# Attention with relative positions and a quantised feed-forward on one NeuronCore: query rows copied on chip, and two additions moved to VectorE

## The reference

```python
x = x + attention(ln(x))          # q.k/4 + rel_bias_h + rel_bias_w, softmax, times v, times Wp, plus bp
t = ln(tokens(x))
xq = round(clip(t / mean(alpha_a1), -8, 7));  wq1 = round(clip(w1 / alpha_w1, -8, 7))
h = clip(gelu(xq @ wq1.T * alpha_w1 * mean(alpha_a1) + b1), -10, 10)
hq = round(clip(h / mean(alpha_a2), -8, 7));  wq2 = round(clip(w2 / alpha_w2, -8, 7))
out = tokens(x) + (hq @ wq2.T * alpha_w2 * mean(alpha_a2) + b2)
```

## Time and profile before

| | us |
|---|---|
| median of 3 runs (lowest, highest) | 999.8 (998.39, 1002.08) |
| the profiled execution: its own time | 1000.03 |
| the profiled execution: span of the trace | 998.2 |
| a unit of attention in the steady state | 53.33 |
| a group of the feed-forward in the steady state | 13.15 |

### The profile page before, as it was taken

The page is one execution under the profiler, slowest core; times in us unless marked ns, Lnnn a source line. Parts: engine busy times, 40 slices in busy tenths (PEclk is TensorE's granted clock), DMA queues, the critical chain, the costliest instruction groups (busy, mean ns, idle before and its releaser), DMA issues. The chain is left out here.

```text
span 998.2 us, 17173 instructions
## 1 busy us (share of the span) xinstructions
PE 876.6 (88%) x6808; PEld 465.2 (47%) x6808; DVE 738.4 (74%) x1488; ACT 559.2 (56%) x654; POOL 379.8 (38%) x199
## 2 busy tenths in 40 slices
PE   4798579378999999999999999999999999787864
PEld 2465356133444444444444444444444443365643
DVE  7665455178888888888888888888888884059994
ACT  1322333104676766666666666676676667537663
POOL 1456520054435252626252525345252222013442
PEclk9899655558999999999999999999999999879896
DMA  5676449889929375674839291929485000323311
GB/s 143 185 217 224 170 120 240 248 213 190 188 54 194 79 166 106 131 143 105 166 78 191 55 196 42 207 50 197 76 171 101 12 12 11 121 95 111 118 41 48
DMA packets 65682, 130.18 MB, mean 130 GB/s; under 512 B 9465, under 2 KB 45306, under 8 KB 57146
## 3 DMA queue, kind: packets, MB, share of 16 engines
q1 hardware_dynamic: 65602, 129.08, 55.7%
HBM read 89.73 MB, written 34.60 MB: 125 GB/s over the span
## 5 line engine op out<-in xcount | busy, mean ns | idle before, releaser
L1060 DVE TENSOR_REDUCE at_piece_neg<-at_r_ps 128x1 f32<-128x512 f32 x768 | 492.0, 687 | 94.9 <-PE at_r_ps L901 94.5
L1024 ACT ACTIVATE at_probs<-at_s_ps 128x1024 f32<-128x1024 f32 x384 | 372.1, 1021 | 187.2 <-PE at_s_ps L925 187.1
L834 POOL COPY op_mix_q<-op_mix_q 2x4096 f16<-2x4096 f16 x48 | 172.7, 3597 | 372.1 <-ACT op_mix_q L1030 372.1
L901 PE MATMUL at_r_ps<-op_mix_k,op_mix_q 128*128 128x256 f16 (+1 forms) x1920 | 287.8, 258 | 19.0 <-DVE at_piece_neg L1060 15.3
L901 PEld LDWEIGHTS at_r_ps<-op_mix_k,op_mix_q 128*128 128x128 f16 x1920 | 150.4, 100 | 284.0 <-DVE at_piece_neg L1060 197.9
L925 PE MATMUL at_s_ps<-op_mix_q,op_mix_k 128*128 128x512 f16 x768 | 227.5, 380 | 1.1 <-ACT at_probs L1024 0.7
L939 PE MATMUL at_o_ps<-at_probs,op_v_u 128*32 128x512 f32 x1536 | 204.2, 604 | 0.0
L218 POOL MEMSET op_mix_q<- 2x10240 f32 x12 | 103.5, 8626 | 25.5 <-DVE op_v_u L1194 25.5
L925 PEld LDWEIGHTS at_s_ps<-op_mix_q,op_mix_k 128*128 128x128 f16 x768 | 73.8, 98 | 17.3 <-ACT at_probs L1024 8.3
L1030 ACT ACTIVATE op_mix_q<-at_r_ps 2x512 f16<-2x512 f32 x96 | 51.5, 581 | 39.2 <-PE at_r_ps L914 38.7
L690 DVE TENSOR_TENSOR op_mix_q<-rb_b_ps,op_mix_q 128x512 f16<-128x512 f32 (+1 forms) x36 | 29.5, 863 | 58.3 <-ACT op_mix_q L677 58.3
(11 more groups left out here) (121 smaller groups left out, 702.6 us busy)
## 6 DMA issues: line engine op xcount, KB each, us to landing
op_mix_q<-qk_parts SPq DMA_DIRECT2D x48, 640.0 KB, 10.9
op_mix_q<-bias_parts SPq DMA_DIRECT2D x120, 120.0 KB, 10.2
bias_parts<-op_mix_q SPq DMA_DIRECT2D x12, 1024.0 KB, 7.1
op_mix_q<-bias_parts SPq DMA_DIRECT2D x72, 128.0 KB, 10.3
qk_parts<-op_mix_q SPq DMA_DIRECT2D x24, 256.0 KB, 2.4
v_rows<-pr_v_st SPq DMA_DIRECT2D x8, 768.0 KB, 4.4
op_mix_k<-qk_parts SPq DMA_DIRECT2D x48, 128.0 KB, 13.3
op_v_u<-v_rows SPq DMA_DIRECT2D x12, 512.0 KB, 14.3
```

What stands on the lines that cost most here:

```text
L834: pool.tensor_copy(rows[:, 1:, :, :], rows[:, 0:1, :, :].to_broadcast([2, ops.VARIANTS - 1, 2, GROUP])).then_inc(max_spread, 1)
L901: last = pe.matmul(r_bank("piece", at)[:, first % GROUP:first % GROUP + n], mix_q[owner.buf][:, variant, j, qt * P:(qt + 1) * P], mix_k[ow ...
L1024: act.activation(probs[n % PRING][:, 2 * pair:2 * pair + 2, :], s_ps[pair][:, :, :], ACT.Exp).then_inc(exp_done, 1)
L1060: dve.tensor_reduce(piece_neg[half][:, i:i + 1], r_bank("piece", at)[:, :], AX_X, ALU.max, negate=True).then_inc(reduced, 1)
```

## The change

The query rows of `mix_q` are loaded from DRAM into variant 0 alone, with semaphores of their own (`q_in`), and POOL copies 64 rows x 4096 elements from there to each of the variants 1 to 4 (`copy_queries`), for unit 0 in the relative-bias phase, for unit 1 at the start of attention, ahead of its first spread, and for unit u+2 in unit u, two copies ahead of each of its last two spreads. PE waits for these copies where it waits for the loads. In the feed-forward phase the additions of b2 and of the residual are made by DVE: res behind the scaling (L1386), y_b as the last work of a group's turn.

```diff
-    N_LOADS = 4 + 4 + 1 + 2 * (4 + 5)
+    N_LOADS = 4 + 1 + 2 * (4 + 5)
...
+    def copy_queries(self, pool, image, i, variants):
+
+        pool.wait_ge(self.q_in[i], (image + 1) * 4 * 16)
+        for variant in variants:
+            pool.tensor_copy(self.mix_q[i][0:self.A_AT, variant, :, :], self.mix_q[i][0:self.A_AT, 0, :, :]).then_inc(self.q_copied, 1)
...
         for r, part in enumerate((0, 0, 1, 1)):
-            src = q_or_k(0, part).unsqueeze(1).to_broadcast([HD, self.VARIANTS, QUAD * SEQ])
-            sp.dma_start(self.mix_q[i][r:self.A_AT:4, :, :, :].rearrange("p v j t -> p v (j t)"), src).then_inc(self.loaded[i], 16)
+            sp.dma_start(self.mix_q[i][r:self.A_AT:4, 0, :, :].rearrange("p j t -> p (j t)"), q_or_k(0, part)).then_inc(self.q_in[i], 16)
...
             ops.zero_max(pool, 0)
+            pool.wait_ge(ops.max_zeroed, 1)
+            ops.copy_queries(pool, 0, 0, (1, 2, 3, 4))
...
+            pool.wait_ge(ops.max_zeroed, 1)
             ops.zero_max(pool, 1)
+            pool.wait_ge(ops.max_zeroed, 2)
+            ops.copy_queries(pool, 0, 1, (1, 2, 3, 4))
+            pool.wait_ge(ops.q_copied, 8)
             for pair in range(2):
                 spread_max(Unit(0, 0, 0), 0, pair)
 
             def emit(unit):
+                nxt = unit.after(2)
+                coming = unit.u + 2 < UNITS
                 spread_max(unit, 1, 0)
                 if unit.first:
                     pool.wait_ge(ops.last_stored, 32 * NQUAD)
-                if unit.u + 2 < UNITS:
+                if coming:
                     need(pool, pv_done, unit.u * STEPS)
-                    ops.zero_max(pool, unit.after(2).buf)
+                    ops.zero_max(pool, nxt.buf)
                 spread_max(unit, 1, 1)
+                pool.wait_ge(max_spread, unit.u * 4 + 4)
+                if coming:
+                    ops.copy_queries(pool, nxt.image, nxt.buf, (1, 2))
+                    pool.wait_ge(ops.q_copied, nxt.u * 4 + 2)
                 if not unit.last:
-                    for pair in range(2):
-                        spread_max(unit.after(1), 0, pair)
+                    spread_max(unit.after(1), 0, 0)
+                    pool.wait_ge(max_spread, unit.u * 4 + 5)
+                if coming:
+                    ops.copy_queries(pool, nxt.image, nxt.buf, (3, 4))
+                    pool.wait_ge(ops.q_copied, nxt.u * 4 + 4)
+                if not unit.last:
+                    spread_max(unit.after(1), 0, 1)
...
             pe.wait_ge(loaded[0], 16 * N_LOADS)
+            pe.wait_ge(ops.q_copied, 4)
...
                         pe.wait_ge(ops.max_zeroed, nxt.u + 1)
+                        pe.wait_ge(ops.q_copied, nxt.u * 4 + 4)
...
-            def add_b2(g):
-
-                pool.wait_ge(y_done, g.n + 1)
-                need(pool, res_done, g.n - 1)
-                pool.tensor_tensor(out=y_b[g.s][:, :, :], in0=y[g.s][:, :, :], in1=b2_row[:, :].unsqueeze(1).to_broadcast([P, TILES, C]),
-                                   op=ALU.add).then_inc(yb_done, 1)
-
-            def stage_c(g):
-                pool.wait_ge(scaled, g.n + 1)
-                pool.wait_ge(yb_done, g.n + 1)
-                need(pool, stored[g.s], g.it * 16)
-                pool.tensor_tensor(out=res[g.s][:, :, :], in0=ffn[g.s][:, :, :], in1=y_b[g.s][:, :, :], op=ALU.add).then_inc(res_done, 1)
...
                 last.then_inc(scaled, 1)
+                dve.wait_ge(scaled, g.n + 1)
+                dve.wait_ge(yb_done, g.n + 1)
+                need(dve, stored[g.s], g.it * 16)
+                dve.tensor_tensor(res[g.s][:, :, :], ffn[g.s][:, :, :], y_b[g.s][:, :, :], ALU.add).then_inc(res_done, 1)
+
+            def add_b2(g):
+
+                dve.wait_ge(y_done, g.n + 1)
+                need(dve, res_done, g.n - 1)
+                dve.tensor_tensor(y_b[g.s][:, :, :], y[g.s][:, :, :], b2_row[:, :].unsqueeze(1).to_broadcast([P, TILES, C]), ALU.add).then_inc(yb_done, 1)
...
             residual(FIRST.after(1))
+            add_b2(FIRST)
...
                     stage_c(g.after(-1))
+                if not g.last:
+                    add_b2(g.after(1))
```

More of the change, by code:

```diff
@@ L157, in __init__ @@
         self.loaded = [self.sem(f"loaded{i}") for i in range(3)]
+        self.q_in = [self.sem(f"q_in{i}") for i in range(3)]
+        self.q_copied = self.sem("q_copied")
         early, late = (m[:, :, :, :].rearrange("p v j t -> p (v j t)") for m in self.mix_q[1:])
@@ L1300, in inverse_std @@
                 pool.tensor_tensor(out=rstd[g.s][:, 0, :], in0=var_eps[g.s][:, :], in1=half_neg[:, :], op=ALU.pow).then_inc(pow_done, 1)
-            def add_b2(g):
-                pool.wait_ge(y_done, g.n + 1)
-                need(pool, res_done, g.n - 1)
-                pool.tensor_tensor(out=y_b[g.s][:, :, :], in0=y[g.s][:, :, :], in1=b2_row[:, :].unsqueeze(1).to_broadcast([P, TILES, C]),
-                                   op=ALU.add).then_inc(yb_done, 1)
-            def stage_c(g):
-                pool.wait_ge(scaled, g.n + 1)
-                pool.wait_ge(yb_done, g.n + 1)
-                need(pool, stored[g.s], g.it * 16)
-                pool.tensor_tensor(out=res[g.s][:, :, :], in0=ffn[g.s][:, :, :], in1=y_b[g.s][:, :, :], op=ALU.add).then_inc(res_done, 1)
             inverse_std(FIRST)
             inverse_std(FIRST.after(1))
-            add_b2(FIRST)
             def emit(g):
@@ L1321, in emit @@
                     inverse_std(g.after(2))
[L1322 to L1325, removed]
             each_group(pool, emit)
-            stage_c(LAST)
         @block.vector
@@ L1336, in residual @@
                 dve.wait_ge(proj_done, g.n + 1)
-                need(dve, yb_done, g.n - 1)
                 dve.tensor_tensor(y[g.s][:, :, :], p_ps[:, :, 0:C], x_in[g.s][:, :, :], ALU.add).then_inc(y_done, 1)
@@ L1383, in stage_c @@
                 dve.wait_ge(f_done, g.n + 1)
-                need(dve, res_done, g.n - 1)
                 for t in range(TILES):
```

## The result

| | before | after |
|---|---|---|
| median (lowest, highest), us | 1000.29 (998.39, 1002.08), 4 runs | 1015.24 (1013.93, 1015.49), 4 runs |
| profiled execution: own time, span, us | 1000.03, 998.2 | 1015.49, 1013.5 |
| mean granted clock | 0.916 | 0.921 |

The changed kernel is slower: the ratio is 1.0142, with an interval of 1.013 to 1.0155. The prediction said 1010.5 us, so the sign and the main place were right, and 4.7 us are missing.

The account below looks back on a forecast made before the run. It took DMA as the bound late in the relative-bias phase, PE in attention, DVE in the feed-forward. Its terms summed 1000.0 - 7.1 + 3.6 + 21.5 - 7.4 = 1010.6, stated as 1010.5 us, range 981 to 1022.

Parts of the forecast that it names:

- What bounds each stage: DMA bounds the late relative-bias phase, PE attention, DVE the feed-forward; saved query bytes matter only for unit 0.
- Part 1, fewer query bytes: Ahead of attention, unit 0's load 2.10 MB shorter: gain 9.5 us, between 8.3 and 10.8.
- Part 2, unit 0's copies: Relative-bias phase: POOL copies of 3.60 us delay DVE's large tensor_scalars by up to 9 us; 2.4 sticks out.
- Part 3, the join of step 9: Attention, units 0 to 9: DVE's join stands until POOL's second copy ends, costing PE 2.07 us a unit.
- The join of step 13: Attention, units 0 to 9: DVE's join stands about 0.1 us more, behind the copies of variants 3 and 4.
- Part 3, the clock: Attention: PE taken as the bound at clock 1.00, with no term for a lower clock.
- Part 3, the start of attention: Four copies for unit 1 in a row; DVE's join meets the last: +3.6 us, 0 to 7.
- Part 4, feed-forward: POOL's additions move to DVE, whose stalls there go: -7.4 us, between -3 and -9; a group takes 12.0 us.
- The copies do not hold DVE: Rival for attention's joins: one-input copies do not stall DVE, or end before the join; 983 us, chance 0.18.
- The long copy: Rival: a POOL copy of 64 rows takes 5 us, so the join stands 4.9 us; 1038 us, chance 0.06.
- the half absorbed stall: Rival: DVE's gaps and another order of PE's banks leave 1.0 us a unit in attention; 999 us, chance 0.06.
- does not do what it says: Rival: the DMA queue keeps its time, bound by other traffic; 1018 us, chance counted within the forecast's 0.70.

Follow-up runs that it names:

- e6: Changed kernel with the short query load and POOL copies for unit 0 alone, behind the second quantised matrix; later units load five variants by DMA: 979.21 us.
- e4: Changed kernel with one more wait: POOL makes unit 0's four copies only after DVE has quantised the second weight matrix: 1006.82 us.
- e2: Changed kernel with its feed-forward phase put back to that of the kernel before, so the query copies alone: 1021.53 us.
- e3: Changed kernel with each POOL query copy replaced by a memset of the same elements, leaving variants 1 to 4 zero: 989.06 us.
- e1: Kernel before with only the changed feed-forward phase, its additions on DVE: 992.83 us.
- e5: Changed kernel, all copies kept, POOL's order written around the joins (first order), unit 0's copies behind the second quantised matrix: 986.09 us.
- e7: Changed kernel with each POOL copy of four heads made as two copies of two heads: 1013.27 us.
- e8: Changed kernel, all copies kept, POOL's order rewritten around the joins from measured places (second order), unit 0's copies behind the second quantised matrix: 980.41 us.

## Why the prediction was right, and where it was not

- **What bounds each stage.** As it said: DMA at the start, PE in attention, DVE in the feed-forward. The 12 x 2.10 MB less in the bytes read is there and, but for unit 0's, worth nothing (e6).
- **Part 1, fewer query bytes: mis-sized.** It took 9.5 us, between 8.3 and 10.8, from the bytes at a mean rate. e4, in which nothing else stands in the way, shows 13.2, of which 7.5 are the earlier issue of the store and 5.7 its faster landing. Both factors were off: the stage moved 2.80 MB less, not 2.10, and the traffic that went had run at an estimated 206 GB/s, below the mean of 254.
- **Part 2, unit 0's copies: price right, consequence mis-sized.** A copy took 3.607 us against 3.60 assumed. DVE's large operations stood 9.7 us, just over the bound of 9. What stuck out was put at 2.4 us; it was 7.4 (198.3 in the changed kernel, 190.9 in e4), less the 0.3 us by which e4 was ahead when the loads went out. The step that failed took PE's waiting for cover. DVE's late low parts of the fifth piece held PE back (in the changed kernel PE stood 12.15 us for them), so that it could not work three chunks ahead while ACT waited: in e4 and before ACT takes three chunks in 2.85 us as soon as the store has landed, in the changed kernel ACT starts 2.6 us later and each chunk comes at PE's pace, 3.7 us apart. That is 2.6 + 4.8 = 7.4. The two errors nearly cancel: -7.1 was said, and -13.2 + 7.1 = -6.1 came.
- **Part 3, the join of step 9: right, a little short.** 2.07 us were said, the operation took 1.84 more than before, in all ten units, and the units grew by the whole 1.84. The join of step 13 stood 0.1 in one unit and nothing in the nine others, where 0.1 in each was said. e2 and e3 show the cause: copies alone bring the stall, memsets in their place don't.
- **Part 3, the clock: missed.** Three units lost another 1.63 us each, 4.9 in all, to 3.4 us at the lower clock level. No term of the sum had it: 10 x 1.84 + 3 x 1.63 + 0.1 = 23.4, as between the spreads.
- **Part 3, the start of attention: one copy instead of two.** 3.6 us were said, for one copy met by the join at 227.33, and 0 to 7 as the bounds. The step that failed was the start of the copies: they began 14.8 us after the start of attention and not 11.5, having waited 5.57 us for the query rows. So the join came 7.6 us into the row of copies and not 11.3, in the third and not the last. A copy was left to hold its third operation too: 3.08 + 3.45 us, less twice 0.17, is 6.2, of which 5.8 came through.
- **Part 4, feed-forward: right, with a slip in the sum.** -7.4 said, -7.5 in the ledger, -8.1 in e1 by medians. A group 12.11 against 12.0. The slip: by its own rows the stall of 1.6 in group 2, less one addition of 0.97, is -0.6 and not -0.8, and group 1 has the same stall (1.76 us on L1355) and no term. With both right the sum is about -7.9, which the measurements do not tell from -7.4.
- **The rivals.** "The copies do not hold DVE" would have been 983. Its condition fails in every unit, but its price was good, partly by luck: with 47 of 48 joins cleared and unit 0's copies late, the changed kernel runs in 980.41; the 983 held part 1 at 9.5 and not 13.2. The long copy fell with the 3.607 us, the half absorbed stall with PE's 1.20 us wait, and "does not do what it says" with the 13.2 us of e4.

The 4.7 us between forecast and median lie, by spans, in the start (1.0), in attention's start (2.2) and in the ten units (1.9: the clock's 4.9 less 3.1 for the shorter stalls, and 0.1 for the one join of step 13); the rest, -0.3, is below what is to be told apart.

## What to carry to other kernels

An engine's free time is not enough to take over a copy: what decides is whether, at each instant of it, the other engine has an operation due that such a copy holds (here those that read two SBUF operands, and the large tensor_scalars) and that is on the bound's path. Here the same 48 copies cost 26 us where they met the joins and next to nothing where they did not, for some waits in POOL's program. Write such an order from a measured timeline and look again, since the first new order delays what it was written from (e5); and ask of each byte saved whether its stage waits for bytes, which in this kernel only unit 0's does.

## What the runs showed of the hardware that was not expected

- **A short stall can be followed by the lower clock level.** In every third unit of the changed kernel PE, having stood for about 1.8 us at the join, ran 3.4 us at the 1.2 GHz level, at a price of 1.63 us. e2 had three such stretches too, 168 us apart as here; e4, with the same ten stalls, had two, 222 us apart, and e7 five; e5 had two, behind the two joins of the units that were held longest, 2.05 and 2.63 us. The kernels whose joins were not held in units 1 to 9 (before, e1, e3, e6, e8) had none there. Why not every stalled unit has one was not found.
- **A chain of small operations is caught again by the next copy**: 3.08 + 3.45 us at the start of attention, 0.43 + 1.92 in e7. Between two copies in a row DVE got one small operation through, or none. Splitting the copies gained nothing that can be told apart (1013.27 against 1015.24 us, ratios of 1.0129 and 1.0142 with intervals that overlap).
- **One-input operations can stand too.** The large tensor_scalars stood beside copies and beside memsets alike, while the reductions, which read PSUM, ran at their own 0.69 us inside a copy.
- **A copy's price does not depend on its rows.** 2 rows or 64 of 4096 elements: 3.600 and 3.607 us in the mean. Half the row: 1.909 in the mean, 1.886 in the median.
